# Layer norms and projections by pairs of tiles, PSUM copies on ACT, and the norm's transposes between the projection's products

## The reference

```
x = x + attn_a0(norm(x))      # causal attention, 32 heads of 8, 8 kv heads, rotary
x = x + moe_f0(norm(x))       # top 1 of 4 experts, hidden 1024
x = x + b0(norm(x))           # qkv product, rotary, sum over tokens of k/|k| * v, times q, out product, + input
x = x + moe_f0(norm(x))
x = x + a1(norm(x))           # linear attention, relu q and k, decay
x = x + moe_f1(norm(x))       # top 2 of 8 experts plus a shared expert
x = x + attn_b1(norm(x))      # causal attention, 16 heads of 16, 4 kv heads, rotary
x = x + moe_f1(norm(x))
norm(x) = (x - mean) / sqrt(var + 1e-5) over the 256 features
```

## Time and profile before

| what | value |
|---|---|
| median of three runs | 2199.68 us (2199.32 to 2202.53) |
| the profiled execution | 2207.23 us, its span 2205.4 us |
| PE, PEld, DVE, ACT, POOL busy | 83%, 46%, 51%, 33%, 22% of the span |
| chain of work that ended last | PE 66%, DVE 13%, issue 9%, POOL 3% |
| mean granted clock of PE | 0.888 of full speed |

### The profile page before, as it was taken

How to read it: one execution, slowest core, us unless ns; L and a number is a source line. 1 busy time by engine, 2 the same in 40 slices (tenths; PEclk the granted TensorE clock), 3 DMA queues, 4 the chain that set the end, 5 groups by cost and what they waited for, 6 DMA issues and landing times.

```text
span 2205.4 us, 32805 instructions
## 1 busy us (share of the span) xinstructions
PE 1831.6 (83%) x10372; PEld 1021.5 (46%) x10377; DVE 1119.1 (51%) x2293; ACT 735.0 (33%) x1421; POOL 491.5 (22%) x840
## 2 busy tenths in 40 slices
PE   7899999999399995749999487699468999976992
PEld 4344444443256653535666255376243444444751
DVE  6688888882322216641222456143357888452423
ACT  3277777774011110111111001022033766610210
POOL 2222222221300005530000501500442222133022
PEclk9599999997699996769999697799787999987996
DMA  4241111124100002010000400233222221002322
GB/s 118 68 131 38 38 39 38 38 102 147 45 21 20 24 22 86 1 35 27 21 21 22 155 14 5 88 95 103 62 80 56 38 37 21 2 30 82 101 89 76
DMA packets 97290, 123.34 MB, mean 56 GB/s; under 512 B 19704, under 2 KB 77976, under 8 KB 96408
## 3 DMA queue, kind: packets, MB, share of 16 engines
q1 hardware_dynamic: 87960, 96.67, 15.1%
q0 software_dynamic: 9216, 25.18, 3.5%
HBM read 78.35 MB, written 42.86 MB: 55 GB/s over the span
## 4 chain that ended last, share of the span: by engine, by line
PE 66%; DVE 13%; issue 9%; another core or an unknown queue 4%; POOL 3%; DMA 2%; ACT 1%; SPq 0%; POOLq 0%; DVEq 0%; ACTq 0%
PE psum L1374 12%; PE psum L1024 8%; PE psum L1008 7%; DVE region_a L772 6%; PE psum L1395 6%; PE psum L969 5%; PE psum L1609 5%; PE psum L1581 2%; PE psum L355 2%; POOL y_norm L1269 2%; PE psum L1627 2%; PE psum L1628 2%; PE psum L1812 2%; PE psum L1384 1%
## 5 line engine op out<-in xcount | busy, mean ns | idle before, releaser
L772 DVE TENSOR_REDUCE region_a<-psum 128x1 f32<-128x640 f32 (+7 forms) x576 | 528.5, 954 | 110.2 <-PE psum L974 58.9
L876 ACT ACTIVATE region_w<-psum 128x512 f32<-128x512 f32 x864 | 465.6, 600 | 223.8 <-PE psum L1008 220.4
L1374 PE MATMUL psum<-region_w,region_a 128*128 x608 | 271.8, 600 | 1.4 <-DVE region_a L1450 1.2
L1024 PE MATMUL psum<-region_w,region_a 128*32 128x512 f32 (+3 forms) x2304 | 254.7, 516 | 0.8 <-POOL region_w L699 0.6
L969 PE MATMUL psum<-region_a,y_norm 48*128 48x512 bf16 (+7 forms) x816 | 225.3, 352 | 5.0 <-DVE region_a L772 4.1
L699 POOL TENSOR_SCALAR_AFFINE_SELECT region_w<-region_w 128x512 f32<-128x512 f32 x192 | 122.3, 637 | 459.9 <-ACT region_w L876 455.5
L1269 POOL DMA_INDIRECT y_norm<-result_rows,region_a x64 | 63.3, 989 | 714.6 <-DMA result_rows<-region_a 696.6
L1008 PE MATMUL psum<-y_norm,region_a 51*128 51x512 bf16 (+1 forms) x612 | 206.3, 401 | 6.2 <-DMA y_norm<-region_a 4.3
L1374 PEld LDWEIGHTS psum<-region_w,region_a 128*128 128x128 f32 x608 | 114.2, 193 | 132.4 <-issue 132.4
L1581 PE MATMUL psum<-y_t,region_w 128*128 128x512 f32 (+1 forms) x192 | 101.8, 686 | 73.5 <-DVE ctx L1700 55.4
L1457 DVE TENSOR_TENSOR region_a<-psum,region_a 128x512 f32<-128x512 f32 x76 | 52.7, 693 | 215.5 <-PE psum L1374 215.5
(11 more groups left out here) (189 smaller groups left out, 2605.3 us busy)
## 6 DMA issues: line engine op xcount, KB each, us to landing
region_a<-sorted_rows SPq DMA_DIRECT2D x116, 128.0 KB, 2.0
result_rows<-region_a SPq DMA_DIRECT2D x116, 128.0 KB, 1.7
y_norm<-a_q SPq DMA_DIRECT2D x132, 64.0 KB
sorted_rows<-ctx SPq DMA_DIRECT2D x1, 4992.0 KB, 16.9
y_norm<-b_q SPq DMA_DIRECT2D x36, 128.0 KB
region_w<-in_f_wg SPq DMA_DIRECT2D x1, 4096.0 KB, 13.3
region_w<-in_f_wu SPq DMA_DIRECT2D x1, 4096.0 KB, 13.6
region_w<-in_f_wd SPq DMA_DIRECT2D x1, 4096.0 KB, 14.6
```

What stands on the lines that cost most here:

```text
L772: dve.tensor_reduce(dst, src, AX_X, ALU.max, negate=True).then_inc(self.ring_done.sem, 1)
L876: act.activation(self.p[col % P_RING][:, :, i % 4, :], c.bank[ST_BANKS[s % 3]].rearrange("p (h t) -> p h t", h=GQ), ACT.Exp, scale=self.sc ...
L1024: mm = pe.matmul(c.bank[ACC_BANK][32 * h:32 * h + 32, P * lo:512], self.vp[slot][:, j, :], self.p[col % P_RING][:, h, lo:4, :], start=(j = ...
L1374: mm = pe.matmul(bank[:, :], self.yt[:, f, :], w[:, f, bass.ds(own * self.hidden + 512 * half, 512)], start=(f == 0), stop=(f == FT - 1))
```

## The change

The LayerNorm's DVE and POOL work goes by pairs of tiles: eight steps n instead of four groups g. `finish_vector` is called with a pair; the wait that a tile's addition is complete stands directly ahead of its statistics (`tile_done`). Normalization lags by `norm_lag` pairs: 1, but 3 behind a routed layer. ACT makes all copies from PSUM to `c.yt`, but two that stay on DVE: half f = 1 of the projection's first group and of the norm's last group. The LayerNorm's transposes wait pair by pair. Behind a projection they are issued by the projection's PE part: the norm's group 0 between multiply(2) and multiply(3), the others behind multiply(3). POOL makes two roots of two elements a group instead of one of four; behind a projection and at the start with one group of lag (instead of two), behind a routed layer with two, so that both roots of group 0 stand ahead of the last group's gathers.

```diff
 class LayerNorm: vector
-        def copies(g):
-            dve.wait_ge(self.turned, FT * (NG * k + g + 1))
-            dve.tensor_copy(c.yt[:, 1, 512 * g:512 * g + 512], c.bank[5 + 2 * (g % 2)][:, :]).then_inc(self.yt1, 1)
-        for g in range(NG + 2):
-            if g < NG:
-                self.before.finish_vector(dve, g)
-                statistics(g)
-            if 1 <= g <= NG:
-                normalize(g - 1)
-            if g >= 2:
-                copies(g - 2)
+        def statistics(n):
+            for t in (2 * n, 2 * n + 1):
+                self.before.tile_done(dve, t)
+                dve.bn_stats(c.stats[:, t, :], c.x[:, t, :]).then_inc(self.stat, 1)
+            for t in (2 * n, 2 * n + 1):
+                dve.wait_ge(self.stat, NT * k + t + 1)
+                dve.bn_aggr(c.mv[:, t, :], c.stats[:, t, :]).then_inc(self.aggr, 1)
+        def normalize(n):
+            dve.wait_ge(self.rstd, pairs * k + n + 1)
+            for t in (2 * n, 2 * n + 1):
+                dve.tensor_scalar(c.yn[:, t, :], c.x[:, t, :], c.mv[:, t, 0:1], c.rstd[:, t:t + 1],
+                                  ALU.subtract, ALU.mult).then_inc(self.norm, 1)
+        for n in range(pairs):
+            self.before.finish_vector(dve, n)
+            statistics(n)
+            if n >= lag:
+                normalize(n - lag)
+        for n in range(pairs - lag, pairs):
+            normalize(n)
+        dve.wait_ge(self.turned, FT * NG * (k + 1))
+        dve.tensor_copy(c.yt[:, 1, 512 * (NG - 1):], c.bank[5 + 2 * ((NG - 1) % 2)][:, :]).then_inc(self.yt1_last, 1)
 class LayerNorm: gpsimd (roots(n) on two elements, s = slice(2 * n, 2 * n + 2))
+        lag = 2 if self.before.norm_lag > 1 else 1
+        for g in range(NG + lag):
+            if g < NG:
+                self.before.finish_gpsimd(pool, g)
+            if g >= lag:
+                roots(2 * (g - lag))
+                roots(2 * (g - lag) + 1)
 class LayerNorm: PE
+    def turn(self, pe, g):
+        for q in (0, 2):
+            self.normed(pe, 4 * g + q + 1)
+            for f in range(FT):
...
+                for i in (q, q + 1):
+                    mm = pe.transpose(c.bank[4 + 2 * (g % 2) + f][:, P * i:P * i + P],
+                                      c.yn[:, 4 * g + i, P * f:P * f + P], c.identf[:, :])
+                if q == 2:
+                    mm.then_inc(self.turned, 1)
 class LayerNorm: scalar
+            for f, done in enumerate((self.yt0, self.yt1)[0:2 if g < NG - 1 else 1]):
+                act.wait_ge(self.turned, FT * (NG * k + g) + f + 1)
+                act.activation(c.yt[:, f, 512 * g:512 * g + 512], c.bank[4 + 2 * (g % 2) + f][:, :],
+                               ACT.Copy).then_inc(done, 1)
 class Project: PE
             if g:
                 multiply(g - 1)
+        self.next_norm.turn(pe, 0)
         multiply(NG - 1)
+        for g in range(1, NG):
+            self.next_norm.turn(pe, g)
 class Project: DVE
-        if g + 1 < NG:
-            self.copy(dve, g + 1)
-        for t in range(4 * g, 4 * g + 4):
+        for t in (2 * n, 2 * n + 1):
             dve.wait_ge(self.prod, NT * k + t + 1)
             dve.tensor_tensor(c.x[:, t, :], c.bank[t % 4][:, 0:D], c.x[:, t, :], ALU.add).then_inc(self.added, 1)
-        dve.wait_ge(self.added, NT * k + 4 * g + 4)
+    def tile_done(self, dve, t):
+        dve.wait_ge(self.added, NT * self.k + t + 1)
 class Routing: norm_lag = 3; DVE
         for k, done in enumerate(self.added):
-            for t in range(4 * g, 4 * g + 4):
+            for t in (2 * n, 2 * n + 1):
+                if k:
+                    dve.wait_ge(self.added[k - 1].sem, self.added[k - 1].at(t + 1))
                 dve.scalar_tensor_tensor(out=c.x[:, t, :], in0=self.back[k][:, t, :], scalar=self.weight[k][:, t:t + 1],
                                          in1=c.x[:, t, :], op0=ALU.mult, op1=ALU.add).then_inc(done.sem, 1)
-            dve.wait_ge(done.sem, done.at(4 * g + 4))
```

More of the change, by code:

```diff
@@ L244, in __init__ @@
         self.yt1 = c.shared_sem("ln_yt1")
+        self.yt1_last = c.shared_sem("ln_yt1_last")
+        before.next_norm = self
     def ready(self, eng, g):
+        last = g == NG - 1
         eng.wait_ge(self.yt0, NG * self.k + g + 1)
-        eng.wait_ge(self.yt1, NG * self.k + g + 1)
+        eng.wait_ge(self.yt1, (NG - 1) * self.k + (g if last else g + 1))
+        if last:
+            eng.wait_ge(self.yt1_last, self.k + 1)
     def normed(self, eng, t):
@@ L256, in vector @@
         c, k = self.c, self.k
-        def statistics(g):
-            for t in range(4 * g, 4 * g + 4):
+        pairs, lag = NT // 2, self.before.norm_lag
+        def statistics(n):
+            for t in (2 * n, 2 * n + 1):
+                self.before.tile_done(dve, t)
                 dve.bn_stats(c.stats[:, t, :], c.x[:, t, :]).then_inc(self.stat, 1)
-            for t in range(4 * g, 4 * g + 4):
+            for t in (2 * n, 2 * n + 1):
                 dve.wait_ge(self.stat, NT * k + t + 1)
@@ L283, in gpsimd, with roots @@
+        dve.tensor_copy(c.yt[:, 1, 512 * (NG - 1):], c.bank[5 + 2 * ((NG - 1) % 2)][:, :]).then_inc(self.yt1_last, 1)
     def gpsimd(self, pool):
[L285 to L289, removed]
+        c, k, pairs = self.c, self.k, NT // 2
+        def roots(n):
+            s = slice(2 * n, 2 * n + 2)
+            pool.wait_ge(self.aggr, NT * k + 2 * n + 2)
             pool.tensor_scalar(c.vareps[:, s], c.mv[:, s, 1], LN_EPS, None, ALU.add).then_inc(self.veps, 1)
-            pool.wait_ge(self.veps, NG * k + g + 1)
+            pool.wait_ge(self.veps, pairs * k + n + 1)
@@ L312, in scalar @@
+    def tensor(self, pe):
+        if not self.before.turns_next_norm:
+            for g in range(NG):
+                self.turn(pe, g)
     def scalar(self, act):
@@ L335, in tensor, with copied @@
         c, k = self.c, self.k
+        def copied(f, g):
+            if f == 0:
+                pe.wait_ge(self.ot0, NG * k + g + 1)
+            elif g == 0:
+                pe.wait_ge(self.ot1_first, k + 1)
+            else:
+                pe.wait_ge(self.ot1, (NG - 1) * k + g)
         def turn(g):
@@ L367, in scalar, with vector, finish_vector @@
         for g in range(NG):
[L368 to L372, removed]
-        c, k = self.c, self.k
[L374 to L380, removed]
+            for f, done in enumerate((self.ot0, self.ot1)[0:2 if g else 1]):
+                act.wait_ge(self.turned, FT * (NG * k + g) + f + 1)
+                act.activation(c.yt[:, f, 512 * g:512 * g + 512], c.bank[4 + 2 * (g % 2) + f][:, :],
+                               ACT.Copy).then_inc(done, 1)
+    def vector(self, dve):
+        c, k = self.c, self.k
+        dve.wait_ge(self.turned, FT * (NG * k + 1))
+        dve.tensor_copy(c.yt[:, 1, 0:512], c.bank[5][:, :]).then_inc(self.ot1_first, 1)
+    def finish_vector(self, dve, n):
         c, k = self.c, self.k
-        if g + 1 < NG:
-            self.copy(dve, g + 1)
-        for t in range(4 * g, 4 * g + 4):
+        for t in (2 * n, 2 * n + 1):
             dve.wait_ge(self.prod, NT * k + t + 1)
             dve.tensor_tensor(c.x[:, t, :], c.bank[t % 4][:, 0:D], c.x[:, t, :], ALU.add).then_inc(self.added, 1)
-        dve.wait_ge(self.added, NT * k + 4 * g + 4)
+    def tile_done(self, dve, t):
+        dve.wait_ge(self.added, NT * self.k + t + 1)
     def region_free(self, sp):
@@ L2131, in vector @@
     def vector(self, dve):
-        for g in range(NG):
-            self.before.finish_vector(dve, g)
+        for n in range(NT // 2):
+            self.before.finish_vector(dve, n)
     def gpsimd(self, pool):
```

49 lines of the change are left out of this document (21 added, 28 removed).

## The result

| | median of runs | fastest and slowest | profiled execution | its span |
|---|---|---|---|---|
| before (same chip) | 2201.11 us | 2199.32, 2203.40 | 2207.23 us | 2205.4 us |
| changed | 2166.89 us | 2160.62, 2170.77 | 2160.62 us | 2158.9 us |

The ratio is 0.9834, 95% interval 0.9812 to 0.9857. On the 2199.7 us of the forecast that is 2163.2 (2158.3 to 2168.2), 36.5 us faster. The forecast was 2174.2, 25.5 us faster, in a range from 2165: the sign was right, the size fell short by 11 us, and the range missed it. On a second chip the same kernel gave 0.9817 (0.9799 to 0.9834, 2209.3 before).

The account below looks back on a forecast made before the run. PE carries two thirds of the chain, but at nine norm or end seams nearly everything waits for DVE. Projections 19.6, gathers 4.1, start 0.95, end 0.85: 25.5 us off 2199.7 gives 2174.2, 8-in-10 range 2165 to 2184.

Parts of the forecast that it names:

- The projections: Four seams from projection to logits: DVE freed of copies and PE waits, logits start 4.9 us earlier each, 19.6 in all.
- Past L1150 all is one chain up to POOL's scatter, so the gain stays whole: From the logits' products to the scatter: the 19.6 us won ahead of them is kept, with no further change counted.
- the clock's rival: Full clock in all four projection seams and in b0's and a1's steps behind the logits: 3.7 us more, 2170.5; chance 0.20.
- Gathers: Three seams behind routed stages, last gather to norm: 1.0 (b0), 0.9 (a1), 2.2 (b1), sum 4.1 us, bounds 0.3 to 6.
- Start and end: First norm ends with four transposes instead of eight, 0.95 us; final additions run without waits between blocks of four, 0.85 us.
- Overlap broken by waits: DVE instructions each last their whole length, a pair 2.78 us instead of 2.14; total 2193; chance 0.08.
- Dear power: POOL's root of 2 elements costs as much as of 4, not 0.77 us: 4.2 us less gain, 2178.4; chance 0.18.
- An attention in the other clock: An attention starts at half clock: one unit more costs 25.5 us at most, 2199.7 or above; chance 0.05.
- the likeliest one: The forecast as summed, 2174.2, within 2171.5 to 2177 at chance 0.45; with bounds on latency and clock, 2168 to 2181.

Follow-up runs that it names:

- a_order: Changed kernel with PE's old order, all of the norm's transposes behind all of the projection's products; ratio to the kernel before 0.9825.
- b_copies: Kernel before with ACT making all copies from PSUM but two, groups of four and PE's order kept; ratio to the kernel before 0.9898.
- a_dvecopies: Changed kernel with all f=1 copies back on DVE, pairs and PE's new order kept; ratio to the kernel before 0.9944.
- b_warm2: Kernel before with 26 unread transposes ahead of the norm's group 2 transposes, in PE's 4.2 us idle time behind each projection; ratio 0.9964.
- b_warm: Kernel before with 26 unread transposes behind each projection, placed one group too late, behind PE's idle time; ratio to the kernel before 0.9996.
- a_unit: Changed kernel with 26 unread transposes in attention a0's last unit, ahead of step 10's wait for row maxima; ratio to the kernel before 0.9794.
- a_first: Changed kernel with 23 unread transposes in PE's gaps ahead of attention a0's first unit; ratio to the kernel before 0.9816.
- a_delay: Changed kernel with the gathers of both top-two stages held until the shared expert has added its last rows; ratio to the kernel before 0.9952.

## Why the prediction was wrong in size

**The projections: right.** 4.9 us forecast for the start of the logits, 4.93 to 4.95 measured eight times in two profiles. Its parts too: pair 2.16 (2.14), root 0.74 (0.77), last transposes at full clock. DVE's line, not PE's order, makes the number (a_order, b_copies, a_dvecopies).

**The step that failed** is the sentence "Past L1150 all is one chain up to POOL's scatter, so the gain stays whole", with the clock's rival built on it. Both clocks were worked out for the last transposes (0.35 a seam) and not for the products of the logits right behind them: their change of length was put at nothing, without a reason. L1150 ran its 3.59 us at 0.52 of the clock; at full clock it takes 1.90, and b_warm2 (three seams) and b_warm (four) get that without any other part of the change. This is 6.8 us. The short gaps in the changed kernel were forecast, and so was that they would hold the clock; with L1150 in it the rival would have been 25.5 + 3.7 + 6.8 = 36.0 less 1.4, since the start that I took (4.9) already lies near the full clock's: 34.6, or 2165.1. The Trainium skill (TensorE: Matmul & The Clock Gate, Part 1) calls the full clock something that activity releases. b_warm, three seams of b_warm2 and a_unit agree; a_first did not gain by it, and why single seams fall to half clock behind the same work is open.

**The clock's rival at 0.20 was what happened**, and more widely than it said: 1.8 us in a1 and 0.45 in b0 as forecast, 0.36 in b1, 0.3 and 0.5 before multiply(1), 1.2 in the bodies of b0 and a1 (that the steps before multiply(1) and in these bodies are the clock is argued from its shifted stretches, not shown).

**Gathers:** 5.2 and 6.3 us in the two profiles, 4.1 forecast. The data take 1.8 us or less, not 2.8, and POOL's two roots ahead of b0's last gathers did not make these late: they took 4.9 us where the group took 5.9 before.

**Start and end:** 0.6 instead of 0.95. The additions at the end saved 0.85 as forecast; the shared expert's last products in front of them took 0.5 less, with 5.5 us of half clock among them instead of 6.6.

**The other rivals.** Overlap broken by waits: no, a pair would have shown 2.78. The rule of the Trainium skill (VectorE: DVE Perf Modes, The DRAIN you can't avoid) was read there without its exception: the same section says that an operation that is not held starts earlier, and the trace agrees, with two additions in 0.75 us where one takes 0.42. Dear power: no, 0.74. An attention in the other clock: no; from start to end attention a0 took 0.9 us less and 2.4 more in the two profiles, b1 0.2 less and 0.6 more. But its premise was wrong: in the kernel before not every later unit of a0 ran at full clock; the last one ran mostly at half clock, which is where a_unit gained:

```profile
504.50:535.30 30.80, 28.39 (x118) 5.59 (x118) 0.55 (x2) 14.71 (x28) 2.77 (x5) 0.50 0.03 14
```

**The range** had its lower end, 2165, where the clock's 3.7 us lie below the likeliest one's own 2168, although the same row of the clock spoke for every product in the stretch: up to the scatters the clock gave 9.4 (6.8 and 2.6).

## What to carry to other kernels

When a change takes away an idle stretch of PE ahead of matmuls, count everything that PE does next at both clocks, up to the next long wait, and first of all the long products. Ask for each part which engine's line ends last: here ACT's copies and the pairs each gave about half, by way of DVE, and the reordered PE program nothing. Where an engine must idle 3 us ahead of PE-bound work, matmuls that nobody reads can be worth a try (a_unit: 26 transposes, after which the projection started 11.7 us earlier, 5 to 9 us in the ratios), but only a run tells where they hold the clock: b_warm2 lost it in one seam of four, a_first gained nothing.

## What the runs showed of the hardware

While POOL issues gathers, PE's signals come late: in the changed kernel DVE, idle since 2096.87, started its addition at 2128.86, though the products it waits for were over at 2107.57 and the clock had fallen behind them, and with no gathers beside them the wait was gone (a_delay). PE's signals in the first 10 us of the gathers were prompt. Whether other engines' signals are held up too isn't shown: between 2112 and 2128 none of DVE or ACT was waited for. What holds PE's up (the descriptors that POOL writes, or the gathers' own signals) wasn't tried. The two profiles of the changed kernel differ by 3.7 us at the end through this alone.
